# Moving the first sequence's output projection, residual and statistics from the output stage into the end of attention

## The reference, cut to what matters

```python
x = x + attn_a(layernorm(x))
x = x + ffn(layernorm(x))
x = x + attn_b(layernorm(x))      # the change lies at the end of this line
x = x + ffn(layernorm(x))
```

```python
probs = softmax(q @ k.T * scaling)                      # 32 heads
w = probs[:, :, 0] - lam * probs[:, :, 1]               # pairs of heads, 16 left
attn = w @ v
attn = attn * rsqrt(mean(attn * attn, axis=-1) + EPS) * subln_g
attn = attn * (1.0 - LAMBDA_INIT)
return attn.reshape(b, s, 256) @ Wo
```

## Time and profile before

| | |
|---|---|
| median of 3 runs | 9218.43 us (9218.42 to 9221.2) |
| the profiled execution, its own time | 9219.39 us |
| its span, first to last instruction | 9217.7 us |
| TensorE matmul, busy | 7818.7 us (85%) |
| VectorE, busy | 7231.6 us (78%) |
| ScalarE, busy | 6194.6 us (67%) |
| GpSimd, busy | 2695.9 us (29%) |
| granted TensorE clock, mean | 0.919 of full |

### The profile page before, as it was taken

The page is one execution under the profiler, slowest core; times in us unless marked ns, Lnnn a source line. Parts: engine busy times, 40 slices in busy tenths (PEclk is TensorE's granted clock), DMA queues, the critical chain, the costliest instruction groups (busy, mean ns, idle before and its releaser), DMA issues. The chain is left out here.

```text
span 9217.7 us, 163388 instructions
## 1 busy us (share of the span) xinstructions
PE 7818.7 (85%) x65408; PEld 2845.9 (31%) x65408; DVE 7231.6 (78%) x9490; ACT 6194.6 (67%) x11410; POOL 2695.9 (29%) x3046
## 2 busy tenths in 40 slices
PE   6799877998779987799877998779987799777997
PEld 4222342223422234222342223422234222342223
DVE  5899558995589955899558995689955899558995
ACT  4499644995449954499544995449955499554995
POOL 3223242232413324133241332413324133241332
PEclk9799987999879998799987999979999799887998
DMA  0100001000010000100001000010000100001000
GB/s 28 42 23 23 10 10 42 23 23 10 10 42 23 23 10 10 42 23 23 11 9 42 23 23 15 6 42 24 22 16 4 45 23 19 19 1 45 23 19 19
DMA packets 216826, 204.98 MB, mean 22 GB/s; under 512 B 105782, under 2 KB 141110, under 8 KB 216054
## 3 DMA queue, kind: packets, MB, share of 16 engines
q1 hardware_dynamic: 216060, 194.46, 7.3%
HBM read 123.83 MB, written 67.37 MB: 21 GB/s over the span
## 5 line engine op out<-in xcount | busy, mean ns | idle before, releaser
L1240 DVE TENSOR_REDUCE mfull<-ps 128x1 f32<-128x1024 f32 x4096 | 4695.3, 1214 | 296.3 <-PE ps L1169 289.9
L1320 ACT ACTIVATE work<-ps 128x512 f32<-128x512 f32 x8192 | 4386.0, 597 | 349.3 <-PE ps L1191 227.6
L1169 PE MATMUL ps<-kop,qop 48*128 48x512 bf16 x8192 | 2609.4, 402 | 170.0 <-DMA kop<-scratch 110.4
L1209 PE MATMUL ps<-work,vbuf 128*32 128x256 f32 x32768 | 2624.4, 392 | 116.9 <-ACT hh L1340 116.9
L1191 PE MATMUL ps<-qop,kop 51*128 51x512 bf16 x8192 | 2490.1, 384 | 0.0
L1209 PEld LDWEIGHTS ps<-work,vbuf 128*32 128x32 f32 x32768 | 654.4, 108 | 1801.7 <-ACT work L1320 886.9
L1191 PEld LDWEIGHTS ps<-qop,kop 51*128 51x128 bf16 x8192 | 483.0, 93 | 1650.6 <-ACT work L1320 1583.5
L1269 POOL CAST mpart<-mfull 128x32 bf16<-128x32 f32 x128 | 26.8, 209 | 2615.0 <-DVE mfull L1240 2435.9
L1287 POOL TENSOR_TENSOR work<-work,none 128x16 f32<-128x16 f32 x128 | 371.5, 2902 | 1019.2 <-ACT work L1329 1019.2
L263 PE MATMUL ps<-ident,hh 128*128 128x128 f32 x1024 | 200.6, 373 | 508.7 <-DVE hh L233 508.6
L1169 PEld LDWEIGHTS ps<-kop,qop 48*128 48x128 bf16 x8192 | 479.6, 94 | 450.0 <-DVE mfull L1240 321.8
(11 more groups left out here) (163 smaller groups left out, 9198.6 us busy)
## 6 DMA issues: line engine op xcount, KB each, us to landing
qop<-scratch SPq DMA_DIRECT2D x512, 64.0 KB
scratch<-work SPq DMA_DIRECT2D x32, 768.0 KB, 3.5
scratch<-hh SPq DMA_DIRECT2D x32, 768.0 KB, 3.5
kop<-scratch SPq DMA_DIRECT2D x256, 96.0 KB
vbuf<-in_x SPq DMA_DIRECT2D x9, 2048.0 KB, 8.4
qop<-scratch SPq DMA_DIRECT2D x512, 32.0 KB
kop<-scratch SPq DMA_DIRECT2D x256, 64.0 KB
out<-x SPq DMA_DIRECT2D x64, 256.0 KB, 2.1
```

The costliest lines, as they stand in the source:

```text
L1169: pe.matmul(ps[:, b + n, :], qop[r:r + KQ, s, i, t * P:(t + 1) * P], kop[r:r + KQ, s, i, half(n)], start=True, stop=True).then_inc(s_ms, 1)
L1209: mm = pe.matmul(ps[VW * i:VW * (i + 1), OB, cols], vp[:, b, t, (G * gl + i) // 2, :], prob[:, u % PS, i, cols], start=t == 0 and part == ...
L1240: v.tensor_reduce(mfull[:, g % 2, r // ROWS, i * T + t:i * T + t + 1], ps[:, b:b + NB, :].rearrange("p b n -> p (b n)"), AX.X, ALU.max).th ...
L1320: act.activation(prob[:, u % PS, hl, :], ps[:, EB[slot % len(EB)], :], ACT.Exp, scale=scale).then_inc(s_ex, 1)
```

## The change

`features`, `project`, `residual` and `statistics` become functions used by both stages. For sequence 0 they now run in `diff_attention`: at output step `j` TensorE issues, behind `turn_output(j)`, the two transposes of tile `j` into bank 2 and `project(0, j - 1)` into bank 3, and `project(0, 7)` after its last step. The copy out of PSUM for sequence 0 (`keep_features`) is on VectorE now, in the loop that has `combine`, and residual and statistics stand there too. Before the first of these steps TensorE also waits for all of GpSimd's `early` work. `diff_output` keeps sequence 1 alone: its transposes for the first half of the heads go directly behind `turn_output`, without the second half's, into four banks in turn, and `project` uses bank 3. ScalarE's copy there waits until both halves of a tile have been turned. No instruction is added or dropped but for the engine of eight copies in each pair.

```diff
@@ diff_attention, TensorE
                             if output_step(e) == 0:
                                 pe.wait_ge(s_mts, GROUPS)
+                                pe.wait_ge(s_ch, LINKS * 2 * T)
                             turn_output(pe, output_step(e))
+                            if output_step(e) >= 1:
+                                pe.wait_ge(s_we[0], output_step(e))
+                            for c in range(C):
+                                features(pe, 0, output_step(e), c, 2)
+                            if output_step(e) >= 1:
+                                project(pe, 0, output_step(e) - 1)
+                    project(pe, 0, T - 1)
@@ diff_attention, VectorE
                     for j in range(T + 2):
                         if j < T:
                             combine(v, j)
+                            keep_features(v, j)
                         if 1 <= j <= T:
                             mean_square(v, j - 1)
+                            residual(v, 0, j - 1)
                         if j >= 2:
                             normalise(v, j - 2)
+                            statistics(v, 0, j - 2)
@@ diff_output, TensorE
+                    def turned(t, c):
+                        pe.wait_ge(s_an, c * T + t + 1)
+                        if t >= 4 and c == 0:
+                            pe.wait_ge(s_we[1], t - 3)
+                        features(pe, 1, t, c, 4 + t % 4)
                     for t in range(T + 3):
                         if t < T:
                             turn_output(pe, T + t)
-                            for c in range(C):
-                                features(0, t, c)
-                        if 1 <= t <= T:
-                            project(0, t - 1)
+                            turned(t, 0)
                         if 2 <= t < T + 2:
-                            for c in range(C):
-                                features(1, t - 2, c)
+                            turned(t - 2, 1)
                         if t >= 3:
-                            project(1, t - 3)
+                            project(pe, 1, t - 3)
@@ diff_output, VectorE (sequence 0's residual and statistics gone)
-                        if 2 <= t < T + 2:
-                            residual(0, t - 2)
-                        if 3 <= t < T + 3:
-                            statistics(0, t - 3)
                         if 4 <= t < T + 4:
-                            residual(1, t - 4)
+                            residual(v, 1, t - 4)
@@ diff_output, ScalarE
-                    for t in range(T + 2):
-                        if t < T:
-                            keep(0, t)
-                        if t >= 2:
-                            keep(1, t - 2)
+                    for t in range(T):
+                        act.wait_ge(s_wt[1], min(t + 3, T) + t + 1)
+                        src = ps[:, 4 + t % 4, 0:D].rearrange("p (c n) -> p c n", c=C)
+                        act.copy(aT[:, 1, :, t * P:(t + 1) * P], src).then_inc(s_we[1], 1)
```

More of the change, by code:

```diff
@@ L1049, in normalise, with features, project, keep_features @@
                             rr[:, j, :][:, :, None].to_broadcast([P, HV, LD]), ALU.mult).then_inc(s_an, 1)
+        s_wt, s_we, s_wm, s_wx = ([sem(f"do_{n}{b}") for b in range(PB)] for n in ("wt", "we", "wm", "wx"))
+        def features(pe, b, t, c, bank):
+            pe.transpose(ps[:, bank, c * P:(c + 1) * P], attended[:, b, t, c * P:(c + 1) * P],
+                         ident[:, :]).then_inc(s_wt[b], 1)
+        def project(pe, b, t):
+            pe.wait_ge(s_we[b], t + 1)
+            if t >= 1:
+                pe.wait_ge(s_wx[b], t)
+            for c in range(C):
+                mm = pe.matmul(ps[:, 3, 0:D], aT[:, b, c, t * P:(t + 1) * P],
+                               wo[:, c, :], start=c == 0, stop=c == C - 1)
+            mm.then_inc(s_wm[b], 1)
+        def keep_features(v, t):
+            v.wait_ge(s_wt[0], C * (t + 1))
+            v.tensor_copy(aT[:, 0, :, t * P:(t + 1) * P],
+                          ps[:, 2, 0:D].rearrange("p (c n) -> p c n", c=C)).then_inc(s_we[0], 1)
+        def residual(v, b, t):
+            tt = T * b + t
+            v.wait_ge(s_wm[b], t + 1)
+            v.tensor_tensor(x[:, tt, :], x[:, tt, :], ps[:, 3, 0:D], ALU.add).then_inc(s_wx[b], 1)
+        def statistics(v, b, t):
+            tt = T * b + t
+            v.wait_ge(s_wx[b], t + 1)
+            v.bn_stats(st[:, tt, :], x[:, tt, :])
         def diff_attention():
@@ L1353, in diff_output @@
         def diff_output():
-            s_wt, s_we, s_wm, s_wx = ([sem(f"do_{n}{b}") for b in range(PB)] for n in ("wt", "we", "wm", "wx"))
             with nc.Block() as block:
@@ L1358, in _ @@
                 def _(pe):
[L1359 to L1371, removed]
-                        for c in range(C):
-                            mm = pe.matmul(ps[:, 2 + b, 0:D], aT[:, b, c, t * P:(t + 1) * P],
-                                           wo[:, c, :], start=c == 0, stop=c == C - 1)
-                        mm.then_inc(s_wm[b], 1)
+                    def turned(t, c):
[3 more added lines that the diff above has]
+                        features(pe, 1, t, c, 4 + t % 4)
                     for t in range(T + 3):
@@ L1408, in _ @@
                             normalise(v, T + t - 2)
-                        if 2 <= t < T + 2:
-                            residual(0, t - 2)
-                        if 3 <= t < T + 3:
-                            statistics(0, t - 3)
                         if 4 <= t < T + 4:
-                            residual(1, t - 4)
+                            residual(v, 1, t - 4)
                         if t >= 5:
-                            statistics(1, t - 5)
+                            statistics(v, 1, t - 5)
                 @block.gpsimd
```

13 lines of the change are left out of this document (removed).

## The result

The changed kernel took 9230.6 us in the median of 20 runs (9222.3 to 9248.9) against 9218.4 us of the kernel before in its 20 runs beside them (9208.7 to 9230.9). The ratio is 1.0016, with a 95% interval of 1.0010 to 1.0023: slower by 0.16%, where some 9 us less were forecast. The profiled execution of the changed kernel took 9248.94 us, that of the kernel before 9219.39 us; the former is the longest of the 20, so a difference read from these two traces is larger than that of the medians.

The account below looks back on a forecast made before the run. TensorE's queue was taken to set the pace among attention's exponentials, a TensorE-VectorE ring the output stage. Attention 10.0 us longer, output stage 11.3 shorter: -1.3 us per pair, some -10 for eight pairs, so 9209 us, range 9182 to 9240.

Parts of the forecast that it names:

- What attention gains in work: Attention, TensorE's queue: eight pairs of transposes and seven projections add 7.9 us per pair, at most 10.7; 8.1 taken.
- rival D: Attention: TensorE runs ahead of ScalarE and covers the moved work; 9.4 us per pair faster, 9144 us; chance 0.05.
- The tail behind `project(0, 7)`: Attention's end: residual, normalises and statistics on VectorE after the last projection make attention 1.9 us longer per pair.
- VectorE's added work: Attention: 24 instructions of about 0.4 us fit VectorE's free time and cost nothing; otherwise about 10 us a pair.
- the output stage's tail: Output stage, from the last `turn_output` through the last statistics: 10.8 us taken, 10.0 at full clock, 14 at half.
- head: Output stage's start until the fourth `turn_output`: 5.7 us.
- the pass without a residual: Output stage, pass 3, with no residual to wait for: 4.6 us taken, 3.75 at full clock, 4.9 at half.
- three passes: Output stage, passes 4 to 6: 3 x 4.8 = 14.4 us taken; each 3.8 at full clock, 5.2 at half.
- Rival B: Output stage: clock stays at half, passes 5.2 us, stage 39 to 40; kernel 24 us slower, 9243 us; chance 0.15.
- Rival C: Output stage: ring of 3.8 us keeps full clock, stage 32 to 33 us; kernel 32 us faster, 9187; chance 0.22.
- The rule weighed: Output stage: bursts between waits start at low clock; by the page all thinner passes would be at half clock.

Follow-up runs that it names:

- the second set: The kernel before and the changed kernel, both run once more unedited: 9219.2 us (ratio 1.0000) and 9241.0 us (1.0026).

## Why the prediction was wrong

The sign was wrong: 9209 us forecast, 9230.6 measured. That this lies inside the stated range of 9182 to 9240 is in part luck, since the range was made from the output stage's clock alone.

**What attention gains in work: right.** 7.9 us by the sum and 8.1 taken, 7.81 measured. TensorE's queue is the path there, ScalarE's idle time grew as forecast from 0.66 to 1.75 us, and rival D fell with it. The tail behind `project(0, 7)` was put at 1.9 us and was 1.93. Together 10.0 forecast, 9.74 measured. VectorE's added work cost nothing that shows: seven steps at 1.08 us and the first step's transposes at 0.22 are 7.8 us, all of TensorE, and eight exponentials took 4.34 us as before.

**The first step that failed: the output stage's tail, taken near full clock.** Forecast 11.3 us, measured 9.3 and 8.7 in the two profiles. By the terms of the sum, in the fourth pair shown above: head 5.7, measured 5.84; the pass without a residual 4.6, measured 4.93; three passes 14.4, measured 13.4; the tail 10.8, measured 13.2 (4512.16 to 4525.39). The tail was taken near full clock because the last projection before the change took 1.10 us. There, two sequences' projections followed each other, and the clock had risen just ahead. With one sequence's projection between waits the last three stayed at half in 14 of 16 pairs. Rival B's mechanism, half clock in a thinner ring, came true in the tail and the first passes. Rival C's came true for a while: from 18 to 28 us into the stage the clock was full in the first five pairs of the first profile, and the pass wholly inside took 3.86 us, but then it fell. With the tail put right the sum is 10.0 - 8.9 = +1.1 us per pair, so this term alone turns the sign; with every touched term as measured it is +0.5 and +1.0 us in the two profiles, 4 to 8 us in all.

**The second: taking every other stage as unchanged.** The sum had no term for them. The medians are 12 us apart in 20 runs each, and 23 in the second set, so some 4 to 8 and 15 to 19 us are left for stages outside the change. Of the 22 us between forecast and measurement the touched stages make 14 to 18, and these the rest. In the profiles the rest is larger, 3 us per pair or 24 us, all of it in local attention and the first feed-forward. In the kernels with added statistics a shift of 0.7 to 3 us per pair drew 12 to 14 us of such a rest after it by the medians, without any of the change's code; their intervals exclude plain addition by little, and for the shift of 0.3 us the interval leaves it open. That it is the changed kernel's whole remainder isn't shown run by run: a run without a profile can't be divided into stages, and both profiled executions of the changed kernel were longer than its median. Why the pairs of the kernel before come to lie at the shorter lengths more often than those of most other kernels is left open.

**The rule weighed.** In both kernels filler in TensorE's waits took the half clock away, and 6.3 and 7.9 us with it. The rule of the Trainium skill, "TensorE: Matmul & The Clock Gate", section "HAM oscillation — how this bites in real kernels", that short bursts of work between waits start at the low clock, agrees with that in part. The page tells it of waits on DMA that are longer than these of about 2 us, and by it every thin pass would be at half clock, where a pass of 3.86 us ran at 1.00.

## What to carry to other kernels

Where the same engine's queue is on the path in both places, moving work from a stage with waits into one without gains only what the waits cost; here 7.9 us of the stage's 47.1 were the clock at half, and filler matmuls in the waits gave 0.4% where the move gave nothing. Make a forecast with a term for the stages that a change doesn't touch: local attention's length here differed by up to 6 us of 133 from pair to pair and by up to 4 in the mean of a profile, with the place of a clock fall, and the change itself was worth less than 1 us. When a change is worth less than 0.2%, compare it stage by stage and by several profiles, since the whole time also measures where the clock happened to fall.

## What the runs showed of the hardware that was not expected

In one execution the same stage has a few distinct lengths: the second layer norm with the first feed-forward took 111.4 to 111.5, 112.7 to 112.9 or 114.4 to 114.5 us, in 96 pairs of twelve profiles, each length with its own place of the clock's fall, and nothing between. Local attention ran from 132.7 to 138.7 us with unchanged code, and nearly as widely in the first pair alone, ahead of every edit (132.8 to 138.7). A kernel with 0.7 us more per pair took 17.6 us more by its median, and in one whose output stage was 7.9 us shorter, local attention was 3.6 us longer in the mean.
